# One tile fewer held as a dense adjacency: eleven dense tiles and fourteen gathered ones

## The chip, the cores and the metric

The kernel runs on one core of one Trainium2 chip. The metric is the time of one execution in microseconds of device time, median over several runs. Everything is one program: one launch, five engines (TensorE, VectorE, ScalarE, GpSimd and SyncE) that run their own instruction streams in order and wait for each other on semaphores.

## The reference

There are 3125 nodes with 256 features and 100,000 edges, each with a source, a destination and one of 4 relation types, sorted by destination. Destinations are drawn as 3125 u^2 with u uniform, so low node numbers have many edges and high ones few. What is computed, cut to what matters:

```python
X = layernorm(x)
for l in range(4):                                   # graph layers
    h = einsum('ni,rio->rno', X, W[l])               # 4 relations
    msg = h[etype, src] / max(count[dst, etype], 1)
    out = segment_sum(msg, dst) + X @ root[l] + bias[l]
    X = elu(layernorm(out) * gamma[l] + beta[l]) + X
x = x + X
x = x + mixture_of_experts(layernorm(x))             # 8 experts, the best 2 per node
```

## The kernel before, in words

The nodes are split in T = 25 tiles of TN = 125 nodes. For one tile of destinations the kernel sums source features per relation into a PSUM area of 2 x 128 partitions (the two halves of the features) x 500 columns (125 nodes x 4 relations). It has two ways to do this.

**Dense tiles** are the first NEAR = 12 tiles (line 27), which have most edges. In layer 0 their adjacency is built: 25 groups of 5 nodes per tile, each group from some slots of 128 edges. For a slot, VectorE and ScalarE make two one-hot matrices, and one matmul (`pair`, lines 1850 to 1861) multiplies them into PSUM; ScalarE copies a finished group out (line 1296). Finished tiles are stored to DRAM, and in the layers after they are loaded again in five parts each (SyncE, 625 KB a load). A tile then takes T = 25 dense steps a layer (`dense_step`, line 1872): for each tile of sources, 4 matmuls of 500 columns (line 1888; two feature halves, and a high and a low f16 part of the features).

**Far tiles** are the others. Their edges are cut in chunks of 128. For a chunk GpSimd gathers the 128 source rows of 1 KB each from DRAM by an indirect DMA (line 1421) into a ring of GS = 12 slots; VectorE makes one-hot windows for 5 chunks at a time (line 1508); TensorE does 4 matmuls, as wide as the nodes that the chunk can touch times 4 (`chunk`, lines 1895 to 1911). A slot's next gather waits until the chunk that used it is done. In layer 0 there is also one matmul per chunk that counts edges (`count`, line 1837).

How many slots and chunks a tile gets is fixed when the program is built, from the expected number of edges plus four standard deviations (`capacity`, and `self.CH`, `self.groups` in `Near.__init__`). A test at the start (`tests`) looks whether the real edges fit; if not, a second program (`DenseShape`, `dense_scalar`, `dense_tensor`) that holds all 25 tiles dense runs in place of the first. With this input the first one ran.

After a tile, of either kind, follow a scaling on VectorE (line 1601, `finish`), a split in high and low parts (lines 1312, 1523), a transpose of the tile's own features (line 1772), the relation matmuls (6 of line 1923 and 24 of line 1927), the norm and the ELU (`post`, `end`), and the new features go to DRAM (`xstore`). The gathers of a layer start when all tiles of the layer before are stored. In layer 3 the routing to the experts shares the order: per tile, GpSimd also does two scatters (line 1436).

**The order of work** on every engine is written by a planner (`Near.steps`), which keeps its own clock for each engine. The costs that bear here, in its microseconds: a dense step 0.9 on TensorE, a chunk 0.21, the relations 3.4, and a gather

```python
rows[q] = run("pool", 1.4) + 10.0      # line 537: when the rows of chunk q can be used
gather(q + GS)                         # asked for when chunk q is ordered
```

In `pick` it takes, in this order: ready jobs (relations, transposes, routing), the next chunk if it believes its rows and window there and an accumulator free, in layer 0 the next pair or count, and else the next dense step. The engines then follow this order whatever the real durations are. In layer 0 pairs run at most one tile ahead of the dense steps (line 570) and far tiles have one of the accumulator pairs to themselves; later there are three pairs for both kinds.

In `order`, the first dense tile of a layer goes through the source tiles in the order 0-4, 10-14, 15-19, 20-24, 5-9 (`groups_of`), and waits for each of them to be finished in the layer before.

Of the kernel before, what the change touches and what calls it, by code (L numbers as in the profile page):

```python
# [23 lines left out]
GD = 5  # L24
GPT = TN // GD
W = TN * R
NEAR = 12
GS = 12
OW_ = 3
FIVE = 5  # L30
# [14 lines left out]
BATCH = 4  # L45
# [31 lines left out]
S8 = 8  # L77
# [2557 lines left out]
def dense_scalar(e, a, c, m, s):  # L2635
    TD = c.TD
# [9 lines left out]
    for i in range(0, 2 * c.PT, 4):  # L2646
        n = 128 * min(4, 2 * c.PT - i)
# [7 lines left out]
    e.sem_inc(s["evac"], 4)  # L2655
    e.wait_ge(s["eg"], 32)
    e.wait_ge(s["prep"], c.prep["gp_sub"])
    regs = [e.alloc_register(f"er{TD}_{i}") for i in range(BATCH)]
    for t in range(TD):
        if t >= 2:  # L2660
            e.wait_ge(s[f"store{t % 2}"], 16 * (t // 2))
        rows = m.RA[:, 5 * (t % 2):5 * (t % 2) + 5, :].rearrange("p a b -> p (a b)").rearrange(
            "p (k q) -> p k q", q=W)
        for i in range(GPT):
            if i % BATCH == 0:
                n = min(BATCH, GPT - i)
                e.reg_load(regs[0:n], m.egrow[0:1, GPT * t + i:GPT * t + i + n])
            e.wait_ge(s["slot_free"], e.snap(regs[i % BATCH], min_val=1, max_val=c.P) + S8)
            e.activation(rows[:, :, 20 * i:20 * i + 20], m.bank((GPT * t + i) % 4, 0, W).rearrange(
                "p (q k) -> p k q", k=T), ACT.Copy).then_inc(s["evac"], 1)  # L2670

    for what, l, i in c.order:
# [14 lines left out]
        elif what == "end" and l + 1 < L:  # L2687
            t = c.done[i][1]
# [5 lines left out]
        elif what == "split":  # L2694
            n = 512 if i < E8 else 256
# [7 lines left out]
        elif what == "xo" or (what == "ra" and i + 2 < T):  # L2703
            n = i if what == "xo" else i + 2
# [371 lines left out]
def dense_tensor(e, a, c, m, s):  # L3076
    TD = c.TD
# [12 lines left out]
    e.wait_ge(s["tab"], 32)  # L3090
    e.wait_ge(s["vs"], math.ceil(c.PT / 2))
    e.wait_ge(s["prep"], c.prep["b1t"])
    regs = [e.alloc_register(f"pr{TD}_{i}") for i in range(3 * BATCH)]
    n_os = 0
    for p0 in range(0, c.P, BATCH):
        n = min(BATCH, c.P - p0)
        for w in range(3):
            at = w * c.PT * 128 + p0
            e.reg_load(regs[BATCH * w:BATCH * w + n], m.tabrow[0:1, at:at + n])
        for i in range(n):  # L3100
# [3 lines left out]
            if p % 2 == 0:  # L3104
                n_os += (p % 14 in OSG) + ((p + 1) % 14 in OSG and p + 1 < c.P)
                e.wait_ge(s["oc"], min(p + 2, c.P))
                e.wait_ge(s["os"], n_os) if n_os else None
                last = 2 * BATCH + min(i + 1, n - 1)
                e.wait_ge(s["evac"], e.snap(regs[last], min_val=1, max_val=c.G + 1))
            e.matmul(m.PS[:, bass.ds(clear, 2)], m.OS[:, p % S8, :], m.Z[:, :], start=True, stop=False,  # L3110
                     skip_group_check=True)
            e.matmul(m.PS[:, bass.ds(at, W)], m.OS[:, p % S8, :], m.OC[:, p % S8, :], start=False, stop=False,
# [171 lines left out]
```

## Time and profile before

| | us |
|---|---|
| median of 3 runs | 2614.72 |
| lowest and highest | 2608.05, 2615.36 |
| span of the profiled execution (first to last instruction) | 2581.8 |
| busy in it: TensorE | 2075.7 |
| busy in it: VectorE | 1572.2 |
| busy in it: GpSimd | 1253.4 |
| busy in it: ScalarE | 818.3 |

For the profiled execution the profile gives its span only; a full time of its own isn't listed. The median is 32.9 us above the span.
### The profile page before, as it was taken

The numbers are of one execution on the slowest core, as the hardware profiler recorded it, in microseconds if no ns is written. First come the engines' busy times: TensorE is split into PE (matmuls) and PEld (weight loads), VectorE is DVE, ScalarE is ACT, GpSimd is POOL, SyncE is SP. The second block draws the span as 40 slices with busy tenths as digits, with TensorE's granted clock in tenths as the row PEclk, the third lists the DMA queues.
The fourth block names the chain that finished last, engine by engine and source line by source line (L and its number), as shares of the span: only waits on it lengthen the run. The fifth ranks groups of instructions, "written<-read, shape, count | busy, mean of one in ns | idle before, by whom it ended". The sixth has DMA issues, their size and how long they took to land. (4 is left out here: it accounts for less than half of the span.)

```text
span 2581.8 us, 46238 instructions
## 1 busy us (share of the span) xinstructions
PE 2075.7 (80%) x16327; PEld 1296.1 (50%) x16327; DVE 1572.2 (61%) x4475; ACT 818.3 (32%) x1674; POOL 1253.4 (49%) x1223
## 2 busy tenths in 40 slices
PE   0576788787879889898889888898987988774992
PEld 0334455454545455555545545454554645454992
DVE  5976677575656356566553656566364766575665
ACT  1564556454456011111111212111011111123992
POOL 2124333544430266666716666662665656752441
PEclk9988899988889899899989999999997999986996
DMA  5698333444432487666637867765775655532335
GB/s 144 187 273 256 115 112 115 133 123 125 122 112 98 145 256 233 219 210 210 187 113 249 257 210 240 236 218 158 230 231 165 181 163 169 179 101 64 95 94 178
DMA packets 211755, 445.56 MB, mean 173 GB/s; under 512 B 40819, under 2 KB 137088, under 8 KB 209733
## 3 DMA queue, kind: packets, MB, share of 16 engines
q1 hardware_dynamic: 138357, 274.65, 34.6%
q0 software_dynamic: 61408, 156.79, 20.1%
q10 hardware_dynamic: 11760, 11.08, 1.7%
q8 instruction: 141, 2.31, 0.4%
q14 instruction: 89, 0.73, 0.1%
HBM read 338.14 MB, written 103.90 MB: 171 GB/s over the span
## 5 line engine op out<-in xcount | busy, mean ns | idle before, releaser
L1421 POOL DMA_INDIRECT n_BIG<-n_xd,n_SIDX x1080 | 1110.9, 1029 | 1091.2 <-PE n_PS L1907 501.3
L1888 PE MATMUL n_PS<-n_BIG 125*128 125x500 f16 x4800 | 1196.8, 388 | 69.3 <-issue 45.3
L1888 PEld LDWEIGHTS n_PS<-n_BIG 125*128 125x128 f16 x4800 | 441.1, 100 | 508.7 <-issue 142.0
L1907 PEld LDWEIGHTS n_PS<-n_OW,n_BIG 128*128 128x128 f16 x4320 | 256.3, 99 | 204.6 <-issue 68.9
L1907 PE MATMUL n_PS<-n_OW,n_BIG 128*128 128x84 f16 (+21 forms) x4320 | 303.5, 201 | 51.5 <-issue 41.6
L1927 PE MATMUL n_PS<-n_BIG,n_tabs 128*128 128x256 f16 x2400 | 299.3, 280 | 19.4 <-issue 18.9
L1601 DVE TENSOR_TENSOR n_ST<-n_PS,n_INVB 128x500 f32<-128x500 f32 x200 | 199.9, 1041 | 158.4 <-issue 47.6
L1927 PEld LDWEIGHTS n_PS<-n_BIG,n_tabs 128*128 128x128 f16 x2400 | 239.7, 101 | 62.9 <-issue 29.0
L1627 DVE SCALAR_TENSOR_TENSOR n_U<-n_PS,n_cw,n_BI 125x256 f32<-125x256 f32 x100 | 48.2, 482 | 334.9 <-PE n_PS L1927 161.3
L1296 ACT ACTIVATE n_BIG<-n_PS 128x500 f16<-128x500 f32 x300 | 164.3, 578 | 195.5 <-PE n_PS L1859 93.6
L1312 ACT ACTIVATE n_tabs<-n_ST 128x1000 f16<-128x1000 f32 x100 | 103.8, 1038 | 358.8 <-DVE n_ST L1601 192.3
L1508 DVE TENSOR_TENSOR n_OW<-n_io,n_tabs 128x460 f16<-128x460 f16 (+14 forms) x216 | 140.8, 657 | 119.4 <-PE n_PS L1907 59.7
L1323 ACT ACTIVATE n_U<-n_U 125x256 f32<-125x256 f32 x100 | 41.4, 414 | 506.6 <-issue 268.3
L1859 PE MATMUL n_PS<-n_BIG,n_tabs 128*128 128x500 bf16 (+4 forms) x590 | 140.8, 346 | 66.3 <-ACT n_BIG L1296 25.8
L1495 DVE TENSOR_SCALAR n_BIG<-n_io,n_tabs 128x500 bf16<-128x500 f16 (+4 forms) x590 | 154.4, 312 | 63.5 <-PE n_PS L1859 59.9
L1523 DVE TENSOR_TENSOR n_tabs<-n_ST,n_tabs 128x1000 f16<-128x1000 f32 x100 | 120.1, 1201 | 45.2 <-ACT n_tabs L1312 25.9
L1303 ACT ACTIVATE n_XT<-n_PS 128x500 f16<-128x500 f16 x100 | 58.7, 587 | 257.3 <-remote 139.8
L1441 POOL DMA_INDIRECT n_yg<-n_BIG,n_IDX x56 | 64.3, 1148 | 113.7 <-DVE n_BIG L2083 113.1
L1923 PE MATMUL n_PS<-n_RL,n_XT 128*128 128x256 f16 x600 | 88.5, 286 | 38.3 <-issue 21.5
L1277 ACT ACTIVATE n_tabs<-n_io,n_tabs 128x125 bf16<-128x125 f16 x294 | 93.2, 390 | 74.4 <-PE n_PS L1859 69.5
L1859 PEld LDWEIGHTS n_PS<-n_BIG,n_tabs 128*128 128x128 bf16 x590 | 56.8, 104 | 112.5 <-issue 38.0
L1923 PEld LDWEIGHTS n_PS<-n_RL,n_XT 128*128 128x128 f16 x600 | 57.6, 101 | 60.2 <-issue 24.2
(271 smaller groups left out, 2252.9 us busy)
## 6 DMA issues: line engine op xcount, KB each, us to landing
n_BIG<-n_a SPq DMA_DIRECT2D x175, 625.0 KB
n_a<-n_BIG SPq DMA_DIRECT2D x12, 3125.0 KB
n_xg<-n_tabs SPq DMA_DIRECT2D x53, 481.9 KB
n_INVB<-n_ind SPq DMA_DIRECT2D x100, 250.0 KB
n_BIG<-n_xd,n_SIDX POOLq DMA_INDIRECT x1080
n_BIG<-in_L_ffn_W_dram SPq DMA_DIRECT2D x32, 512.0 KB
n_xd<-n_BIG SPq DMA_DIRECT2D x75, 112.0 KB
n_whl<-n_BIG SPq DMA_DIRECT2D x16, 512.0 KB
```

What stands on the lines that cost most here:

```text
L1296: e.activation(rows[:, :, 20 * g:20 * g + 20], m.bank(4 + c.unit_of["block", i], 0, W).rearrange("p (q k) -> p k q", k=T), ACT.Copy).then_ ...
L1312: e.activation(m.SH[i % 2 if l else 0][:, 0, :, :, 0:TN], m.ST, ACT.Copy).then_inc(s["shi"], 1)
L1421: e.indirect_dma_start(m.GR[:, g % GS, :], None, m.XD[l % 2][:, :], bass.IndirectOffsetOnAxis(ap=m.SIDX[:, i:i + 1], axis=0)).then_inc(s[f ...
L1495: e.tensor_scalar(m.OC[i % S][:, at], m.io[:, at], m.VS[:, i:i + 1], None, ALU.is_equal).then_inc(s["oc"], 1)
L1508: e.tensor_tensor(m.OW[:, i % OW_, 0:n * wide].rearrange("p (c w) -> p c w", w=wide), m.io[:, 0:wide].unsqueeze(1).broadcast_to([128, n, w ...
L1523: e.tensor_tensor(lo, m.ST, hi, ALU.subtract).then_inc(s["slo"], 1)
L1601: ins = e.tensor_tensor(m.ST[:, h], m.bank(2 * p + h, 0, W).rearrange("p (n r) -> p r n", r=R), m.INVB[:, k, :].rearrange("p (n r) -> p r ...
L1859: e.matmul(m.bank(4 + c.unit_of["block", g])[:, at], m.OS[b % 3][:, i % 4, :], m.OC[i % S][:, at], start=(j == 0), stop=(j + 1 == c.groups ...
L1888: ins = e.matmul(m.bank(2 * p + h, 0, W), m.xps[l % 2][0:TN, part, D * k + 128 * h:D * k + 128 * h + 128], m.RA[0:TN, c.slot_of(n), W * (k ...
L1907: ins = e.matmul(m.bank(2 * p + h, at, c.width[q]), m.GR[:, g % GS, D * part + 128 * h:D * part + 128 * h + 128], ow, start=(first == 0 an ...
L1923: e.matmul(out, m.XT[:, f % 2, 2 * x + h, :], m.RH[:, l % 2, w, h, :], start=(x + w + h == 0), stop=False)
L1927: ins = e.matmul(out, sums[:, x, h, r, :], m.WH[:, l % 2, w, h, r, :], start=False, stop=(x == 1 and h == 1 and r == R - 1))
```

## The change

`NEAR` is 11. Tile 11 (nodes 1375 to 1499) is then a far tile: its pairs, block copies, store, loads and dense steps are not made, and chunks, gathers, windows and counts for it are. All shapes and the whole order follow from the constant, as the planner runs anew. The rest of the diff is in the second program, which isn't run with this input: its register loads in batches become single loads of a value.

```diff
-NEAR = 12
+NEAR = 11
...
-    regs = [e.alloc_register(f"er{TD}_{i}") for i in range(BATCH)]
...
-            if i % BATCH == 0:
-                n = min(BATCH, GPT - i)
-                e.reg_load(regs[0:n], m.egrow[0:1, GPT * t + i:GPT * t + i + n])
-            e.wait_ge(s["slot_free"], e.snap(regs[i % BATCH], min_val=1, max_val=c.P) + S8)
+            at = GPT * t + i
+            e.wait_ge(s["slot_free"], e.value_load(m.egrow[0:1, at:at + 1], min_val=1, max_val=c.P) + S8)
...
-    regs = [e.alloc_register(f"pr{TD}_{i}") for i in range(3 * BATCH)]
+    regs = [e.alloc_register(f"pr{TD}_{i}") for i in range(2 * BATCH)]
...
-        for w in range(3):
+        for w in range(2):
...
-                last = 2 * BATCH + min(i + 1, n - 1)
-                e.wait_ge(s["evac"], e.snap(regs[last], min_val=1, max_val=c.G + 1))
+                last = 2 * c.PT * 128 + p0 + min(i + 1, n - 1)
+                e.wait_ge(s["evac"], e.value_load(m.tabrow[0:1, last:last + 1], min_val=1, max_val=c.G + 1))
```

## Rows read from the trace of the kernel before

**Rows 1.** The page, part 1: busy us, share of the span, instructions.
```profile
PE 2075.7 (80%) x16327; PEld 1296.1 (50%) x16327; DVE 1572.2 (61%) x4475; ACT 818.3 (32%) x1674; POOL 1253.4 (49%) x1223
```

**Rows 2.** The page, part 2: busy tenths in 40 slices of the span.
```profile
PE   0576788787879889898889888898987988774992
...
POOL 2124333544430266666716666662665656752441
```

**Rows 3.** Stretches: from:to, us, busy us (instructions) per engine, granted clock, DMA share, GB/s.
```profile
150.00:865.00 715.00, 587.63 (x4180) 352.10 (x4179) 453.37 (x1395) 365.84 (x808) 266.76 (x258) 0.91 0.47 142
900.00:1312.00 412.00, 367.83 (x2917) 221.38 (x2916) 247.10 (x597) 60.09 (x93) 267.83 (x259) 0.96 0.69 214
1364.00:1778.00 414.00, 366.81 (x2948) 220.91 (x2947) 246.96 (x584) 77.23 (x110) 268.44 (x259) 0.99 0.74 231
1821.00:2316.00 495.00, 421.24 (x3193) 253.62 (x3191) 292.62 (x898) 75.22 (x136) 312.37 (x299) 0.92 0.58 176
...
795.00:838.00 43.00, 38.30 (x226) 21.75 (x227) 29.32 (x90) 26.96 (x58) 0.00 (x0) 0.98 0.29 105
```

**Rows 4.** Groups by line: instructions, busy us, mean ns, idle before and releaser.
```profile
L1421 POOL DMA_INDIRECT n_BIG<-n_xd,n_SIDX x1080 | 1110.9, 1029 | 1091.2 <-PE n_PS L1907 501.3 <-issue 242.0 <-DMA n_xd<-n_BIG 207.0
...
L1436 POOL DMA_INDIRECT n_xg<-n_tabs,n_INVA x38 | 47.3, 1244 | 44.2 <-DVE n_INVA L1724 32.6 <-issue 11.3 <-ACT n_tabs L1357 0.3
```

**Rows 5.** Timeline of GpSimd: start us, us, instruction, idle before and releaser.
```profile
1349.82 0.95 POOL L1421 DMA_INDIRECT n_BIG<-n_xd,n_SIDX  x1 [48.93 <-DMA n_xd<-n_BIG]
1351.08 0.95 POOL L1421 DMA_INDIRECT n_BIG<-n_xd,n_SIDX  x1 [0.30 <-issue]
...
1807.15 0.94 POOL L1421 DMA_INDIRECT n_BIG<-n_xd,n_SIDX  x1 [40.09 <-DMA n_xd<-n_BIG]
```

**Rows 6.** Waits of GpSimd, 900 to 1312 us: total us, times, longest.
```profile
POOL n_BIG L1421 <- PE n_PS L1907: 53.2, 52, 4.6
```

**Rows 7.** Timeline of TensorE where layers 1 and 2 end and layer 2 begins.
```profile
1312.42 0.25 PE L1907 MATMUL n_PS<-n_OW,n_BIG 128*128 128x16 f16 x4
1312.52 6.07 PE L1888 MATMUL n_PS<-n_BIG 125*128 125x500 f16 x28
...
1318.65 3.54 PE L1888 MATMUL n_PS<-n_BIG 125*128 125x500 f16 x16
...
1325.30 5.23 PE L1888 MATMUL n_PS<-n_BIG 125*128 125x500 f16 x24
...
1347.00 17.77 PE L1888 MATMUL n_PS<-n_BIG 125*128 125x500 f16 x72 [6.99 <-DVE n_BIG L1555]
1364.60 0.26 PE L1907 MATMUL n_PS<-n_OW,n_BIG 128*128 128x32 f16 x4
...
1777.64 0.25 PE L1907 MATMUL n_PS<-n_OW,n_BIG 128*128 128x16 f16 x4
```

**Rows 8.** Timeline of TensorE where layer 3 ends.
```profile
2290.46 2.69 PE L1888 MATMUL n_PS<-n_BIG 125*128 125x500 f16 x12
...
2298.38 1.44 PE L1923 MATMUL n_PS<-n_RL,n_XT 128*128 128x256 f16 x6 [4.33 <-DVE n_tabs L1523]
2299.61 5.04 PE L1927 MATMUL n_PS<-n_BIG,n_tabs 128*128 128x256 f16 x24
...
2304.90 1.40 PE L1907 MATMUL n_PS<-n_OW,n_BIG 128*128 128x108 f16 x24
...
2315.20 0.68 PE L1907 MATMUL n_PS<-n_OW,n_BIG 128*128 128x108 f16 x16
```

**Rows 9.** Timeline of TensorE where layer 0 ends and layer 1 begins.
```profile
847.68 2.78 PE L1927 MATMUL n_PS<-n_BIG,n_tabs 128*128 128x256 f16 x24
850.30 20.43 PE L1888 MATMUL n_PS<-n_BIG 125*128 125x500 f16 x96
...
882.01 4.35 PE L1888 MATMUL n_PS<-n_BIG 125*128 125x500 f16 x10 [6.90 <-DVE n_BIG L1555]
```

## The prediction

> **What bounds the kernel now.** I began with busy time per engine [rows 1]: TensorE 80%, GpSimd 49%, no engine full. The slices say where [rows 2]: TensorE is near nine tenths in the graph layers, GpSimd near 6 or 7 tenths in layers 1 to 3. The rest of the argument is about four stretches, one a layer [rows 3]. In layer 0 (150 to 865 us) TensorE is busy 587.63 of 715 us. From first to last chunk of layers 1, 2 and 3 it is busy 367.83 of 412, 366.81 of 414 and 421.24 of 495 us. TensorE sets the pace there, with little idle time. Next I read the costs per instruction [rows 4]: 1080 gathers, 270 a layer, mean 1029 ns. A full queue adds 0.30 us between gathers [rows 5], so 1.33 us each, against 412/270 = 1.53 us per chunk. GpSimd has 13% in hand, no more. Its waits for a chunk to free a ring slot in layer 1 are 53.2 us in 52 waits [rows 6], which is that margin. Last I looked at what TensorE still has to do when a layer's last chunk is done. In layer 1 the last chunk is at 1312.42 and 7 + 4 + 1 dense steps follow it; in layer 2 it is at 1777.64 [rows 7]. In layer 3 the order is reversed: the last three dense steps start at 2290.46 and 15 chunks follow them [rows 8]. So the two streams of each layer finish almost together, and the change takes work out of the one and adds it to the other.
>
> **Counts.** Tile 11 (nodes 1375 to 1499) is expected to hold 100000(sqrt(0.48) - sqrt(0.44)) = 2950 edges. `capacity` gives ceil((2950 + 217 + 32)/128) = 25 chunks, so NCH goes from 270 to 295. Each of its 25 groups has 118 edges, 2 pairs each: 50 pairs of 882 go. Per layer 25 dense steps (100 matmuls) go and 25 chunks (100 matmuls), 25 gathers and 5 windows come (54 to 59). In layer 0, 25 counts come and 25 block evacuations, one tile store and half of the 50 one-hot builds of ScalarE go. SP issues 15 loads of 625 KB fewer; gathers add 100 x 131 KB. These sizes nearly cancel on queues that are not full.
>
> **Layer 0.** Dense steps cost 20.43/24 = 0.85 us each at full clock [rows 9]: 21.3 us. Between 795 and 838 us TensorE did tile 11's 50 pairs beside tile 10's 25 dense steps and two relation groups, each 2.62 us for 24 matmuls (847.68 to 850.30) and about 0.7 for the 6 before: 43 - 21.3 - 6.6 - about 3 of transposes and waits leaves 12 us of pairs [rows 3, 9]. Together 33 us go. A chunk costs 4 x 0.05 us (24 matmuls of 108 columns in 1.40 us, [rows 8]), at 74 columns about 0.15; 25 of them and 25 one-matmul counts of about 0.1 us are 6 to 7 us. Net -26. The far stream of this layer is not the last to end now (GpSimd has nothing to do from 795 to 838, [rows 3]), but it gets a tile longer and needs a turn of its one accumulator pair more, so I leave 2 us for it: **-24**, bounds -32 (nothing of that) and -10 (the far stream ends last). VectorE's 50 one-hots and ScalarE's evacuations lay beside TensorE's work and give nothing more.
>
> **Layers 1 to 3, the mechanism.** TensorE's instructions run in the order that the planner wrote. It believes that a gather takes 1.4 us, takes a chunk as soon as it believes its rows there, and fills all time between with dense steps. So chunks stand about 1.4 planned us apart, whatever the number of dense steps. With 25 chunks more and 25 dense steps fewer, the dense steps run out before the chunks do. From there TensorE has only chunks, at the pace of the gathers. I call the part with dense steps A, the part after them B.
>
> Pace of A: the measured one per chunk, because its filling is unchanged. Length of B with n chunks: 12 are in the ring, so (n - 12) x 1.33 + 10.5 us, where 10.5 is from a gather's start to rows that can be used. The rows bound this only from above: 1349.82 to 1364.60, 14.8 us, with TensorE in dense steps until then [rows 5, 7]; from below by the 0.95 us of the instruction itself. I take 10.5, nearer to the upper row. The Trainium skill ("DMA: Bandwidth & Descriptors", section "Anatomy of one DMA — SWDGE (gpsimd) path") gives 2.0 us and bytes/436e3 us for such a DMA, an estimate of 2.3 us for 131 KB; by it each B would be 8 us shorter and the sum 24 us lower. No row here shows a gather that quick, and I don't use it.
>
> - Layer 1. 24 dense steps before the first chunk, 12 after the last: 264 on 270 chunks, 0.98 a chunk. After: 251 steps last for 257 chunks, A = 257 x 412/270 = 392 us. B has 38 chunks: 26 x 1.33 + 10.5 = 45. A + B = 437, before 412: +25. After the last chunk, now: 1312.5 to the first gather of the next layer at 1349.8, 37.3 us, of which 12 dense steps. From the last dense result it is 1326.3 (the first four of the 24 matmuls from 1325.30) to 1349.8, 23.5 us of scaling, relations, norm, store and load [rows 5, 7]. That chain stays; the 13.8 us ahead of it go. Net **+11**.
> - Layer 2. 23 steps ahead, about 7 behind: 270 on 270. After: 252 steps, 252 chunks, A = 252 x 413/270 = 386; B = 31 x 1.33 + 10.5 = 52; 438 against 413: +25. Tail 1777.7 to 1807.15 = 29.5 becomes 23.5: -6. The last tile to end is now a far one, needed only at dense step 20 of the next layer and not at step 6, so the 6.99 us wait at 1347.00 [rows 7] shrinks; rows then arrive in 12 us and not 15: -3. Net **+16**.
> - Layer 3. 276 steps on the 255 chunks until 2293, 471 us, 1.85 us a chunk (routing shares the order). After: 251 steps on 232 chunks, A = 429; B has 63: 51 x 1.33 + 10.5 = 78, and about 7 scatters of 1.24 + 0.30 us [rows 4] on the same queue, 11, and 4 for waits as in the 15 chunks that end this layer now. 522 against 494 us: +28; the same -3 for the start, and -4 because B's relation groups find their inputs ready. Net **+21**.
>
> **Sum**: -24 + 11 + 16 + 21 = +24 us. The profiled execution has a span of 2581.8 us; its own full time isn't given, and I let the 32.9 us between the span and the median 2614.72 stand. 2605.8 + 32.9 = 2639 us. Own range of this case 2612 to 2668: layer 0 by its bounds, B at 1.25 us a gather with 8 us of latency (-4, -6, -8), or at 1.45 (+4, +5, +8) with A's pace 1% off.
>
> **Rivals.**
> 1. *Other side: TensorE stays the bound everywhere.* Gathers have 13% in hand and grow 9%. If the order still had filling for all chunks, each layer would lose 21.3 us of dense steps and gain 4: -17.5 in layers 1 to 3 at the granted clock, -26 in layer 0, -79 in all, 2536 us. For it: the 53.2 us of ring waits [rows 6]. Against: the planner's own 1.4 us x 295 = 413 us is more than its work in a layer, and layer 3 shows dense work ending first already. It decides if B is under some 15 chunks a layer. 0.12.
> 2. *Break-even.* The far stream doesn't hold layer 0 (-32), B runs at 1.25 us with 8 us of latency and 15 loads fewer let A run 1 to 2% faster (4 to 7 us a layer; the 0.3 us issue gaps inside dense steps are in 412 us): -10 to -35, about 2595. 0.20.
> 3. *The clock.* Before 2298.38 TensorE waited 4.33 us and the next 24 relation matmuls took 5.04 us, against 2.78 elsewhere [rows 8]; after a 6.90 us wait, 10 dense matmuls took 4.35 us, 0.42 each and not 0.21 [rows 9], which is 1.2 and not 2.4 GHz. In B TensorE waits before every chunk. If it is at 1.2 GHz in all of B and into the next layer, 2 or 3 relation groups cost 2.9 us more each and the 24 dense steps that open a layer up to 20 us more, of which the 36 us of chain and first gather hide most: +10 to +20 a layer, 2639 + 45 = 2684. The Trainium skill's page "TensorE: Matmul & The Clock Gate", section "HAM oscillation — how this bites in real kernels", describes this: short bursts between waits for DMA keep starting on the slow clock. By that rule this rival holds; the rows show it after waits of over 4 us, not after 1 us. 0.15.
> 4. *Another program.* If tile 11's edges didn't fit its 25 chunks, the all-dense program would run, some hundreds of us slower. Room for four standard deviations makes it 0.01.
>
> **Chances.** The forecast has 0.52, of which a fifth lies within 0.3% (8 us, about what a measurement of this kernel can tell from no change). Slower: 0.42 + 0.15 + 0.01 + 0.01 of rival 2 = 0.59. Same: 0.10 + 0.06 of rival 2 = 0.16. Faster: 0.12 + 0.13 = 0.25. The range leaves out rival 1 and the upper part of rival 3: 2585 to 2680.
>
> **What would show it.** Layer 0: first gather of layer 1 at 861, not 885. Layers 1 to 3: a run of 35 to 65 chunks with no dense step between at each layer's end, gathers there 1.25 to 1.35 us apart with "issue" before them, TensorE waiting ahead of L1907 and its busy share under a half. First gathers of layers 2 and 3 465 to 480 us after those of 1 and 2 (before 465 and 457). I am wrong if dense steps still stand after the last chunk (rival 1), or if B shows relation groups of 5 us (rival 3).

## The result and the profile after

| us | before | after |
|---|---|---|
| median (4 runs each) | 2615.04 | 2672.95 |
| lowest and highest | 2608.05, 2619.2 | 2666.2, 2680.95 |
| full time and span of the profiled execution | not listed, 2581.8 | 2680.95, 2679.2 |
| granted clock over the span | 0.924 | 0.893 |

The kernel is slower: 2672.95 against 2615.04 us, +57.9, ratio 1.0237 [1.0208, 1.0266]. I had forecast +24. Only 1.75 us lie outside the span of the profiled execution after. So there is no 32.9 us around the span, as I had let stand: the profiled execution before was some 31 us quicker than the timed ones. Why is not shown. It may have run on another chip: e12 below, the same kernel of twelve tiles on a chip where it takes 2582 us, has its first gathers at 885.94, 1350.05 and 1807.69 us, within 1 us of those in that first profile. For the forecast it matters little: scaled to 2615 us, the +24 stays +24.

The busy times after, from the page's parts 1 and 2 and its groups (instructions, busy us, mean ns, idle before):

```profile
PE 2046.9 (76%) x16306; PEld 1292.4 (48%) x16306; DVE 1570.1 (59%) x4439; ACT 794.8 (30%) x1617; POOL 1351.9 (50%) x1323
...
PE   0576878778788889798579898966988898534993
...
L1421 POOL DMA_INDIRECT n_BIG<-n_xd,n_SIDX x1180 | 1210.5, 1026 | 1095.8 <-PE n_PS L1907 549.4
L1888 PE MATMUL n_PS<-n_BIG 125*128 125x500 f16 x4400 | 1102.2, 389 | 39.6 <-issue 31.2
```

Against [rows 1, 2, 4] TensorE works 28.8 us less and the span is 97 us longer. The new thing in the slices are the holes in TensorE's row, "57", "66" and "534", where before there was one, "77": they are the ends of layers 1, 2 and 3. The 100 gathers that came cost as much each as those before (1026 against 1029 ns). Where the holes are, the stretches of the kernel after show (from:to, us, busy us (instructions) of TensorE, its weight loads, VectorE, ScalarE and GpSimd, granted clock, DMA share, GB/s). For layers 1, 2 and 3 the first line is part A, the second part B:

```profile
150.00:865.00 715.00, 567.65 (x4114) 342.44 (x4114) 435.77 (x1324) 341.89 (x750) 289.79 (x283) 0.89 0.48 142
908.00:1298.00 390.00, 344.66 (x2736) 205.49 (x2735) 226.30 (x539) 54.81 (x84) 256.99 (x249) 0.97 0.70 217
1298.00:1358.00 60.00, 25.21 (x277) 20.45 (x274) 33.49 (x89) 8.24 (x14) 36.89 (x35) 0.70 0.40 109
1397.00:1765.00 368.00, 327.06 (x2555) 193.50 (x2553) 209.27 (x501) 64.16 (x91) 243.47 (x236) 0.96 0.74 230
1765.00:1850.00 85.00, 36.48 (x371) 28.30 (x370) 44.42 (x108) 12.96 (x20) 52.16 (x51) 0.68 0.43 126
1889.00:2284.00 395.00, 346.22 (x2617) 204.69 (x2618) 231.00 (x715) 58.68 (x107) 255.57 (x247) 0.93 0.61 185
2284.00:2428.00 144.00, 59.84 (x506) 45.92 (x503) 73.12 (x234) 19.50 (x38) 82.79 (x80) 0.63 0.31 84
```

Parts B exist as forecast: 44, 58 and 73 chunks with no dense step between, TensorE busy 42%, 43% and 42% of 60, 85 and 144 us. But they are longer than the 45, 52 and 93 us that I gave them. In layer 0 [rows 3] TensorE is busy 20 us less in the same 715 us. GpSimd's timeline gives the first gather of each layer; the 885, 1349.82 and 1807.15 us of before [rows 5] have become

```profile
893.33 0.95 POOL L1421 DMA_INDIRECT n_BIG<-n_xd,n_SIDX  x1 [66.78 <-DMA n_xd<-n_BIG]
...
1385.66 0.95 POOL L1421 DMA_INDIRECT n_BIG<-n_xd,n_SIDX  x1 [31.05 <-DMA n_xd<-n_BIG]
...
1877.44 0.95 POOL L1421 DMA_INDIRECT n_BIG<-n_xd,n_SIDX  x1 [31.08 <-DMA n_xd<-n_BIG]
```

Layer 0 is no shorter, and each period from first gather to first gather is longer: 492.3 for 464.9, 491.8 for 457.3. The forecast range for these was 465 to 480.

Inside part B of layer 1, TensorE's timeline (start us, us, instructions, in brackets the idle time before and its releaser):

```profile
1320.59 1.46 PE L1923 MATMUL n_PS<-n_RL,n_XT 128*128 128x256 f16 x6 [5.17 <-issue]
1321.85 4.43 PE L1927 MATMUL n_PS<-n_BIG,n_tabs 128*128 128x256 f16 x24
1326.11 2.22 PE L1907 MATMUL n_PS<-n_OW,n_BIG 128*128 128x100 f16 x48
1339.17 0.60 PE L1772 MATMUL n_PS<-n_idh,n_BIG 125*128 125x125 f16 x4 [10.84 <-issue]
...
1345.61 1.46 PE L1923 MATMUL n_PS<-n_RL,n_XT 128*128 128x256 f16 x6 [5.34 <-DVE n_tabs L1523]
1346.87 3.88 PE L1927 MATMUL n_PS<-n_BIG,n_tabs 128*128 128x256 f16 x24
1350.58 2.44 PE L1907 MATMUL n_PS<-n_OW,n_BIG 128*128 128x84 f16 x48
...
1357.89 0.27 PE L1907 MATMUL n_PS<-n_OW,n_BIG 128*128 128x16 f16 x4 [1.40 <-DMA n_BIG<-n_xd,n_SIDX]
1358.01 7.55 PE L1888 MATMUL n_PS<-n_BIG 125*128 125x500 f16 x24
```

and GpSimd's in the same place:

```profile
1323.38 0.95 POOL L1421 DMA_INDIRECT n_BIG<-n_xd,n_SIDX  x1 [0.31 <-issue]
1326.73 0.95 POOL L1421 DMA_INDIRECT n_BIG<-n_xd,n_SIDX  x1 [2.40 <-PE n_PS L1907]
...
1346.68 0.94 POOL L1421 DMA_INDIRECT n_BIG<-n_xd,n_SIDX  x1 [0.30 <-issue]
1351.17 0.94 POOL L1421 DMA_INDIRECT n_BIG<-n_xd,n_SIDX  x1 [3.55 <-PE n_PS L1907]
```

This is a loop that I had not seen. The far tiles have 25 to 18 chunks each, so in B one ends every 18 or 19 chunks. In layer 1 its transposes stand 1 to 5 chunks later in TensorE's order and its relation group 3 to 8, where the planner believes their inputs ready. In B no dense steps stand between, so TensorE waits 5 to 11 us at the head of its queue for VectorE's chain, with chunks whose rows are there behind it; then it does 12 chunks in a burst (48 matmuls in 2.22 us). For the waits of 5.17 and 10.84 us the profile names no releaser ("issue"); I put them down to VectorE because its split (line 1523, 1319.34 to 1320.54 us) and its scaling (line 1601, 1337.15 to 1339.12 us) end right before them. Meanwhile the ring of 12 slots is full and GpSimd waits 2.40 and 3.55 us for a free one. The gathers in B come 1.63 us apart, not 1.33.

### The profile page after: what moved, and what is told of

It is laid out like the page before. It is cut to its first block and busy times, and to the rows that moved or that the text cites. A ratio compares the mean times of both kernels' runs of the same rounds, so it can differ in the third digit from the quotient of the medians.

```text
span 2679.2 us, 46213 instructions
## 1 busy us (share of the span) xinstructions
PE 2046.9 (76%) x16306; PEld 1292.4 (48%) x16306; DVE 1570.1 (59%) x4439; ACT 794.8 (30%) x1617; POOL 1351.9 (50%) x1323
## 5 line engine op out<-in xcount | busy, mean ns | idle before, releaser
L1421 POOL DMA_INDIRECT n_BIG<-n_xd,n_SIDX x1180 | 1210.5, 1026 | 1095.8 <-PE n_PS L1907 549.4
L1888 PE MATMUL n_PS<-n_BIG 125*128 125x500 f16 x4400 | 1102.2, 389 | 39.6 <-issue 31.2
L1888 PEld LDWEIGHTS n_PS<-n_BIG 125*128 125x128 f16 x4400 | 403.2, 100 | 437.2 <-issue 114.1
L1907 PE MATMUL n_PS<-n_OW,n_BIG 128*128 128x76 f16 (+19 forms) x4720 | 331.4, 203 | 94.3 <-issue 79.1
L1907 PEld LDWEIGHTS n_PS<-n_OW,n_BIG 128*128 128x128 f16 x4720 | 278.1, 100 | 243.2 <-issue 107.3
L1927 PE MATMUL n_PS<-n_BIG,n_tabs 128*128 128x256 f16 x2400 | 318.9, 291 | 23.0 <-issue 22.5
L1927 PEld LDWEIGHTS n_PS<-n_BIG,n_tabs 128*128 128x128 f16 x2400 | 249.5, 105 | 78.8 <-issue 35.9
L1508 DVE TENSOR_TENSOR n_OW<-n_io,n_tabs 128x460 f16<-128x460 f16 (+16 forms) x236 | 152.7, 652 | 144.7 <-remote 83.3
L1296 ACT ACTIVATE n_BIG<-n_PS 128x500 f16<-128x500 f32 x275 | 151.5, 578 | 209.4 <-PE n_PS L1859 120.0
L1441 POOL DMA_INDIRECT n_yg<-n_BIG,n_IDX x56 | 64.5, 1151 | 112.7 <-DVE n_BIG L2083 112.1
L1772 PE MATMUL n_PS<-n_idh,n_BIG 125*128 125x125 f16 x400 | 43.5, 234 | 98.9 <-issue 59.4
L1859 PEld LDWEIGHTS n_PS<-n_BIG,n_tabs 128*128 128x128 bf16 x556 | 53.7, 105 | 125.2 <-issue 66.0
```

The lines of the kernel that those rows point to most:

```text
L1296: e.activation(rows[:, :, 20 * g:20 * g + 20], m.bank(4 + c.unit_of["block", i], 0, W).rearrange("p (q k) -> p k q", k=T), ACT.Copy).then_ ...
L1421: e.indirect_dma_start(m.GR[:, g % GS, :], None, m.XD[l % 2][:, :], bass.IndirectOffsetOnAxis(ap=m.SIDX[:, i:i + 1], axis=0)).then_inc(s[f ...
L1508: e.tensor_tensor(m.OW[:, i % OW_, 0:n * wide].rearrange("p (c w) -> p c w", w=wide), m.io[:, 0:wide].unsqueeze(1).broadcast_to([128, n, w ...
L1859: e.matmul(m.bank(4 + c.unit_of["block", g])[:, at], m.OS[b % 3][:, i % 4, :], m.OC[i % S][:, at], start=(j == 0), stop=(j + 1 == c.groups ...
L1888: ins = e.matmul(m.bank(2 * p + h, 0, W), m.xps[l % 2][0:TN, part, D * k + 128 * h:D * k + 128 * h + 128], m.RA[0:TN, c.slot_of(n), W * (k ...
L1907: ins = e.matmul(m.bank(2 * p + h, at, c.width[q]), m.GR[:, g % GS, D * part + 128 * h:D * part + 128 * h + 128], ow, start=(first == 0 an ...
```

## The experiments

The sets of runs were made on different chips, and the same kernel of twelve tiles took 2615, 2293, 2583.64, 2295.63 and 2582.57 us on them (the first is that of the result). So each ratio is against the kernel before on the same chip, and times are compared only within a set: the first is e1 to e3, the second e4 to e7, the third e8 to e11, the fourth e12 to e15. Chunk stretch means first to last chunk of a layer, tail means last chunk to the next layer's first gather.

**e1: only the second program's edit.** The diff is the kernel after with its constant put back, and e8 and e12 are this kernel again.

```diff
-NEAR = 11
+NEAR = 12
```

> NEAR stays 12; only the second program, which does not run, has the edited register loads. Theory (all of the change comes from the eleventh and twelfth tile): same as before within 0.3%, about 2615 us. Rival (the size or place of the second program's code moves instruction loading of the first): a difference of 10 us or more, either way.

2296.56 us against 2293.08, ratio 1.0017 [1.0006, 1.0027]; again as e8, 0.9999 [0.9987, 1.0012], and as e12, 0.9991 [0.9964, 1.0018]. The edit of the program that doesn't run costs nothing that the three agree on. It is all in the constant.

**e2: gathers of 64 rows**, with the order of the kernel after. Half of each chunk's edges are left out of the sums.

```diff
-            e.indirect_dma_start(m.GR[:, g % GS, :], None, m.XD[l % 2][:, :],
-                                 bass.IndirectOffsetOnAxis(ap=m.SIDX[:, i:i + 1], axis=0)
+            e.indirect_dma_start(m.GR[0:64, g % GS, :], None, m.XD[l % 2][:, :],
+                                 bass.IndirectOffsetOnAxis(ap=m.SIDX[0:64, i:i + 1], axis=0)
...
-                           m.GR[:, g % GS, D * part + 128 * h:D * part + 128 * h + 128], ow,
+                           m.GR[0:64, g % GS, D * part + 128 * h:D * part + 128 * h + 128], ow[0:64],
```

> The changed kernel, same order of work, but each gather fetches the first 64 rows of its chunk and the chunk's matmuls contract over 64 rows and not 128 (half of each chunk's edges are left out of the sums). Theory S (in the stretches without dense steps, B, the pace is that of the gathers, 1.33 to 1.63 us each): a gather gets clearly shorter, B shrinks from 60, 84 and 145 us by a third or more, and the time falls from 2673 to about 2590. Rival H (B's pace is set by relation groups that stand three chunks behind a finished tile and wait for VectorE and ScalarE, with all later chunks queued behind them): the gathers get shorter but B stays within 10 us of 60, 84, 145, and the time is 2650 to 2670.

2411.42 us (two runs), ratio 1.0515 [1.0494, 1.0536]. The manipulation failed: half the rows don't make a gather much shorter on GpSimd. The group of gathers in e2:

```profile
L1421 POOL DMA_INDIRECT n_BIG<-n_xd,n_SIDX x1180 | 1165.0, 987 | 877.7 <-PE n_PS L1907 421.6 <-issue 270.1 <-DMA n_xd<-n_BIG 121.1
```

987 ns against 1033 in e8; the median instruction is 908 ns for 64 rows and 946 for 128. So it says nothing on what cheap gathers would bring. It says that a gather's price on GpSimd hardly depends on its rows, 64 or 128. Part A became slower (1.46, 1.44 and 1.56 us a chunk) on TensorE's side: in layer 1 (799 to 1166 us) TensorE is busy 363.49 of 367 us, and 66.9 us of idle time, in 169 pieces of at most 0.4 us that no wait explains, stand before the weight loads of the 64-row chunks. Why they stand there isn't shown.

**e3: eleven tiles, the planner believes that a gather takes 1.25 us.** It then spends fewer dense steps per chunk, so more are left for later and B is shorter.

```diff
-                    rows[q] = run("pool", 1.4) + 10.0
+                    rows[q] = run("pool", 1.25) + 10.0
```

> The changed kernel with one number of the planner changed: it believes that a gather takes 1.25 us and not 1.4, so it puts fewer dense steps between two chunks and keeps more of them for the end of the layer. No work is added or removed. Theory S: TensorE's part A has slack over the gathers (1.55 us a chunk against 1.33), so it carries more chunks, B shrinks by a third and the time falls by 30 to 50 us, to about 2630. Rival H: B's stalls per finished tile stay, fewer tiles end in B, 10 to 20 us are won. A third (gathers can't go faster than in A now): no change, the waits move into A.

2334.69 us, ratio 1.0173 [1.0141, 1.0205]. That is not told apart from the kernel after (e9, 1.0211 [1.018, 1.0241]). B shrinks from 44, 58 and 73 chunks to 17, 35 and 46, yet layer 1's chunk stretch is 384.4 us as against 383.8 in e9. What B loses comes back in A, as waits for rows. In layer 1 of e3 (785 to 1149 us), waits of TensorE's weight loads and matmuls (total us, times, longest):

```profile
PEld n_PS L1907 <- DMA n_BIG<-n_xd,n_SIDX: 25.7, 26, 3.4
...
PE n_PS L1907 <- DMA n_BIG<-n_xd,n_SIDX: 17.0, 15, 3.2
```

and in e9, with the planner's 1.4:

```profile
PEld n_PS L1907 <- DMA n_BIG<-n_xd,n_SIDX: 3.0, 5, 1.3
...
PE n_PS L1907 <- DMA n_BIG<-n_xd,n_SIDX: 1.9, 4, 0.9
```

So in layer 1 it isn't how the dense steps are spread that costs; the stream of 295 chunks does. (e3 and e9 ran on two chips, on which the kernel before took 2293 and 2296 us.)

**e4: the kernel after again**, as the base of the second set; no edit.

> The changed kernel as it is, timed in the same call as the next three. In the call before, the kernel with twelve dense tiles took 2293 us where it took 2615 at first, and its trace had hardly any idle time before TensorE's instructions that nothing explains. Theory (the loss is in B, part A has room): with less such idle time A runs at the gathers' pace already (1.36 us a chunk), so the loss is larger in per cent: 2293 becomes 2360 to 2400. Rival (the loss came from the idle time of the first chip): the two kernels are within 1% of each other.

2635.53 us, ratio 1.0196 [1.0152, 1.024]. First gathers at 879.3, 1365.3 and 1856.5 us, parts B 56.8, 82.1 and 134.5 us.

**e5: twelve tiles with the planner's 1.25**, the edit of e3 on the kernel of e1.

> Twelve dense tiles and a planner that believes in 1.25 us a gather. Its order leaves 29, 31 and 22 dense steps after the last chunk of layers 1 to 3 (12, 7 and none before). If part A is bound by the gathers already (1.365 us a chunk on this chip against 1.33), nothing is won, and the tail of dense steps adds up to 17 to 24 steps of 0.85 us a layer: 2293 to 2330 us. If A had room, 2270.

2625.02 us, ratio 1.0172 [1.0136, 1.0208]. Now 29, 31 and 22 dense steps stand after the last chunk. The chunk stretches are 408.4, 403.8 and 471.5 us (1.51, 1.50 and 1.75 us a chunk), and what costs are the tails of layers 1 and 2, 50.2 and 52.7 us where the first profile has 37.4 and 29.5. A mismatch of the two streams costs about as much on the other side as the change does on this one.

**e6: eleven tiles, relation groups believed ready 5 us later** (the edit below, at both places where they are asked for), so that they stand later in TensorE's order: in part B of layer 1, 7 to 12 chunks after the end of their tile, not 3 to 8.

```diff
-                    job(max(sums[n], turned[n]), "product", l, n)
+                    job(max(sums[n], turned[n]) + 5.0, "product", l, n)
```

> Eleven dense tiles, and the planner believes the input of a relation group ready 5 us later than before, so in B it stands 6 to 9 chunks after the tile's transpose and not 2 or 3. The number of chunks in B hardly changes (45, 60, 74). Rival H (relation groups too early in the order hold up the chunks behind them and so the gathers): B's gathers come closer to 1.30 us apart, 3 to 6 us are won for each of the 2 to 4 tiles that end in B, 15 to 35 us in all against the changed kernel. Theory S alone (gather supply): within 8 us of the changed kernel.

2645.31 us, ratio 1.0232 [1.0194, 1.0269], beside e4's 1.0196 not told apart. The loop seen in B is real: the gathers there come 1.51, 1.51 and 1.72 us apart for 1.54, 1.64 and 1.97 in e4, and B of layer 3 is 115.0 us for 134.5. But the relations then end later: the tails of layers 1 and 2 are 32.5 and 32.8 us for 27.9 and 28.5, and from layer 3's last chunk to the experts' first matmul it is 57.8 us for 38.2. What the waits of the relation groups cost in B is paid elsewhere when they are moved.

**e7: ten dense tiles**, `NEAR = 10`, 322 chunks.

> Ten dense tiles: 322 chunks a layer, 275 - 25 dense steps. 112, 112 and 130 chunks of layers 1 to 3 and 37 of layer 0 stand after the last dense step, where with eleven it is 44, 58, 73 and none. Theory (a layer's length is its number of chunks at the pace of the gathers, in B 1.4 to 1.7 us, plus 40 us between layers; layer 0 gains nothing more): 27 chunks more a layer cost 27 x 1.4 = 38 us in layers 1 to 3, layer 0 gains at most 10: 100 to 120 us over the changed kernel. Rival (TensorE's work decides and B's stalls are a matter of the order's end only): 20 to 50 us over it.

2777.33 us, ratio 1.0734 [1.0694, 1.0774], 142 us over e4, above what I expected. The parts B have 112, 112 and 130 chunks. New is layer 0: 37 chunks stand behind its last dense step, 60.0 us, and the next layer's first gather is at 913.1 us, for 879.3. There the far stream ends layer 0 for certain; with eleven tiles (e4) its last chunk is 26 us ahead of the last dense step.

**e8 and e9: twelve and eleven tiles on one chip**, each with a profile, no edit beyond e1's.

> Twelve dense tiles (only the second program, which does not run, has the edited loads), for a trace taken beside that of the next kernel. Same as before within 0.3%. Theory: layers 1 and 2 from first gather to first gather as in the first trace (465 and 457 us) or, where TensorE has hardly any unexplained idle time, as in the second (408, 406).

> The changed kernel, beside the one above. Theory: against it, layer 0 gives 5 to 10 us back, layers 1 and 2 (first gather to first gather) are 20 to 35 us longer each, layer 3 up to the start of the experts 5 to 10 us longer; 50 us in all, and more, 70 to 90, if on this chip the part with dense steps has little unexplained idle time, since the gathers then bound both parts.

2294.79 and 2341.61 us, ratios 0.9999 [0.9987, 1.0012] and 1.0211 [1.018, 1.0241]. First gathers of layers 1 to 3 in e8, from GpSimd's timeline:

```profile
792.39 0.94 POOL L1421 DMA_INDIRECT n_BIG<-n_xd,n_SIDX  x1 [112.79 <-DMA n_xd<-n_BIG]
...
1198.69 0.95 POOL L1421 DMA_INDIRECT n_BIG<-n_xd,n_SIDX  x1 [44.04 <-DMA n_xd<-n_BIG]
...
1604.21 0.94 POOL L1421 DMA_INDIRECT n_BIG<-n_xd,n_SIDX  x1 [38.23 <-DMA n_xd<-n_BIG]
```

and in e9:

```profile
785.00 0.94 POOL L1421 DMA_INDIRECT n_BIG<-n_xd,n_SIDX  x1 [61.92 <-DMA n_xd<-n_BIG]
...
1210.31 0.95 POOL L1421 DMA_INDIRECT n_BIG<-n_xd,n_SIDX  x1 [30.14 <-DMA n_xd<-n_BIG]
...
1633.29 0.94 POOL L1421 DMA_INDIRECT n_BIG<-n_xd,n_SIDX  x1 [31.04 <-DMA n_xd<-n_BIG]
```

With spans of 2290.3 and 2340.1 us that is, by layer, -7.4, +19.0, +17.5 and +20.7, in all +49.8. The chunk stretches, divided by 270 and 295 chunks, are the plainest number of the case:

| us per chunk | layer 1 | layer 2 | layer 3 |
|---|---|---|---|
| before, profile of the forecast | 1.53 | 1.53 | 1.83 |
| after, first profile | 1.53 | 1.53 | 1.83 |
| e8, twelve tiles | 1.31 | 1.34 | 1.51 |
| e9, eleven tiles | 1.30 | 1.30 | 1.51 |
| e12, twelve tiles | 1.53 | 1.53 | 1.84 |
| e14, eleven tiles | 1.50 | 1.51 | 1.75 |
| e7, ten tiles (322 chunks) | 1.54 | 1.49 | 1.71 |

The time per chunk hardly changes when dense steps are taken away: it falls by 0 to 5%. On the chip of e8 and e9 TensorE is full where it has dense steps: in part A of layer 1 of e9, 799 to 1132 us, it is busy 328.60 of 333.00 us (1.32 us a chunk). But the order spends about one dense step per chunk there whatever is left of them, and in B only the pace of the gathers counts (1.30 and 1.34 us apart in layers 1 and 2), so what was taken from TensorE is not got back. TensorE's pace in A is the planner's choice of filling; that it nearly equals the gathers' pace in B on this chip is no law.

**e10: twelve tiles, the planner believes that a gather takes 1.46 us.** The opposite edit to e5, from what the others pointed to: spend the dense steps a little earlier, so that none stands behind the last chunk.

```diff
-                    rows[q] = run("pool", 1.4) + 10.0
+                    rows[q] = run("pool", 1.46) + 10.0
```

> Twelve dense tiles and a planner that believes in 1.46 us a gather: 2, 2 and 36 chunks of layers 1 to 3 stand after the last dense step, and no dense step after the last chunk (with 1.4: 12, 7 and none dense steps after, 15 chunks in layer 3). Theory (what costs is a stretch in which one of the two streams runs alone): layers 1 and 2 win 5 to 10 us each at their end, layer 3 loses 10 for 21 chunks more without filling: within 0.5% of before. Rival (only the gathers' pace counts, any wider spacing of the chunks costs its 0.06 us x 270 a layer): 30 to 45 us slower.

2280.51 us, ratio 0.9937 [0.9914, 0.9959]: the only version that beats both kernels. 2, 2 and 36 chunks stand after the last dense step. The first gather of layer 2 is at

```profile
1188.27 0.94 POOL L1421 DMA_INDIRECT n_BIG<-n_xd,n_SIDX  x1 [33.53 <-DMA n_xd<-n_BIG]
```

and so layer 1 takes 399.3 us for 406.3 in e8: its chunk stretch is 5 us longer (359.3) and its tail 12 us shorter (25.8 for 37.5). Layer 2 takes 403.3 us for 405.5, layer 0 ends 3.4 us earlier, and the rest from layer 3 on is 1 us longer.

**e11: eleven tiles, each of the 175 chunks of parts B multiplied four times**, to keep TensorE working there.

```diff
+    for again in range(4 if (l, q) in c.tail else 1):
...
-                           start=(first == 0 and part == 0), stop=False, skip_group_check=True)
+                               start=(first + again == 0 and part == 0), stop=False, skip_group_check=True)
```

> The changed kernel, but every chunk that stands after a layer's last dense step (175 in layers 1 to 3) is multiplied four times and not once, so its edges are counted fourfold. 12 more matmuls of about 90 columns a chunk, 0.5 us, 85 us of work in all for TensorE, in the stretch where it waits. Clock theory (the waits let TensorE fall to 1.2 GHz, relation groups take 4 to 5 us and not 2.8, and this feeds back into the chunks behind them): work in the gaps keeps 2.4 GHz, relation groups in B take 3 us, and the time is the same or up to 15 us less. Rival (the slow clock hides behind the gathers, or the work adds to the chain): 5 to 30 us more than the changed kernel. If TensorE were the bound in B: 85 us more.

2346.87 us, ratio 1.0219 [1.0187, 1.025], not told apart from e9. Part B of layer 1 in e9:

```profile
1132.00:1184.00 52.00, 26.62 (x268) 20.61 (x269) 31.67 (x82) 8.23 (x14) 36.90 (x38) 0.73 0.48 134
```

and in e11:

```profile
1135.00:1184.00 49.00, 42.13 (x729) 38.24 (x726) 30.65 (x76) 7.83 (x13) 36.61 (x37) 0.90 0.49 137
```

The granted clock rises from 0.73 to 0.90, and the parts B are 54, 76 and 121 us for 52, 72 and 120. On this chip neither the clock nor TensorE's work in B sets its length; the gathers, 1.29 us apart in B of layer 1, do. The edit raises both at once, so a small gain by the clock could hide behind the added work. On the chips of the forecast, where the gathers in B wait for TensorE and are 1.63 us apart, it wasn't tried.

**e12 to e15: what holds layer 0.** e12 and e14 are the kernels of twelve and of eleven tiles; e13 and e15 are the same with three of four matmuls left out of 46 dense steps of layer 0.

```diff
+    thin = l == 0 and t >= c.TD - 2 and 0 < kk < T - 1
     for h in range(2):
         for part in range(2):
+            if thin and (h, part) != (1, 1):
+                continue
```

> The kernel with twelve dense tiles again, as the base of the next run on the same chip. Ratio to the kernel before 1.00. Its first gather of layer 1 marks where layer 0 ends (792.4 us on a quicker chip, 885.0 on the first).

> Leaves out part of the computation: in layer 0, the 23 middle dense steps of tiles 10 and 11 do one of their four matmuls, so TensorE has 138 matmuls of 0.213 us (29.4 us) less there, and all else stays: the order, one-hots, copies, windows, the far stream. Theory A, that which my forecast used (TensorE's work is what layer 0 takes): layer 0 and the whole kernel are 27 to 29 us shorter. Theory B (removing TensorE's work there leaves more waits for VectorE, ScalarE and the far stream): 10 to 20 us shorter, and the idle time of TensorE in layer 0 grows by the rest.

> The kernel after again, as the base of the next run on the same chip. Ratio to the kernel before 1.02; its layer 0 ends 6 to 8 us before that of the twelve-tile kernel (7.4 and about 6 in two comparisons), where the forecast had 24.

> The same cut in the kernel after: the 23 middle dense steps of tiles 9 and 10 do one of four matmuls in layer 0, 29.4 us of TensorE's work less. Theory A (work alone): 27 to 29 us shorter than the kernel after. Theory B (in this kernel the far stream with its one accumulator pair, a tile longer, and VectorE's finishes are nearer to being the last of layer 0): the gain is smaller than the same cut brings with twelve tiles, 5 to 15 us. If both cuts bring the same, the far tile more is not what holds layer 0, and what was wrong there is the amount of TensorE's work.

| | median us | ratio to before | last pair of layer 0 | its last dense step ends | first gather of layer 1 |
|---|---|---|---|---|---|
| e12, twelve | 2581.57 | 0.9991 [0.9964, 1.0018] | 835.3 | 866.6 | 885.9 |
| e13, 29.4 us of matmuls fewer | 2575.34 | 0.9966 [0.9949, 0.9984] | 834.0 | 851.6 | 881.9 |
| e14, eleven | 2641.39 | 1.0226 [1.0201, 1.0251] | 836.4 | 869.6 | 888.7 |
| e15, 29.4 us of matmuls fewer | 2626.37 | 1.0164 [1.014, 1.0188] | 831.3 | 851.4 | 883.0 |

(The last dense step is found by counting matmuls along the planned order.) With 29.4 us of TensorE's work out, layer 0 ends (first gather of layer 1) 4.0 us earlier with twelve tiles and 5.7 with eleven. So theory A falls, and e13 gives less than even theory B had. Both cuts bring nearly the same, so the far tile more isn't what holds layer 0 either. The last pair comes within 5.1 us in all four, though e14 and e15 have 50 pairs fewer. (The medians fall by 6 and 15 us. What e15 gains beyond layer 0 lies in layer 2, 475.4 for 484.3 us, where nothing was edited; a layer of one profile varies by that much.) Stretches of e12 with tile 11's pairs (first line) and up to the next layer (second):

```profile
740.00:836.00 96.00, 87.32 (x554) 51.14 (x555) 64.86 (x203) 58.12 (x127) 10.08 (x9) 0.95 0.33 105
836.00:886.00 50.00, 39.48 (x207) 20.40 (x205) 22.42 (x58) 7.40 (x11) 0.06 (x1) 0.92 0.51 144
```

and of e13:

```profile
740.00:836.00 96.00, 80.81 (x513) 47.45 (x511) 66.71 (x210) 61.08 (x133) 12.49 (x12) 0.95 0.34 109
836.00:882.00 46.00, 29.63 (x136) 15.37 (x137) 21.57 (x59) 6.98 (x10) 0.14 (x1) 0.70 0.46 156
```

In the first of these stretches waits came where the work went from. TensorE's waits for ScalarE's copy of a finished block there, e12:

```profile
PEld n_PS L1859 <- ACT n_BIG L1296: 1.5, 4, 0.7
...
PE n_PS L1859 <- ACT n_BIG L1296: 0.3, 1, 0.3
```

and e13:

```profile
PEld n_PS L1859 <- ACT n_BIG L1296: 13.6, 21, 2.0
PE n_PS L1859 <- ACT n_BIG L1296: 6.0, 7, 1.5
```

TensorE is busy 91% of that stretch in e12 and still its work isn't what sets the length: pair, copy, free PSUM and next pair form a loop over TensorE and ScalarE, with the one-hots of VectorE beside it, and the dense steps lay in its gaps. That this loop sets the length is argued from these waits, not shown: e14 and e15 have 50 pairs fewer and no earlier last pair to match.

Behind the last pair it is otherwise. There the cut in the last tile's steps, 14.7 us, comes through: the last dense step ends 15.0 us earlier in e13 and 18.2 in e15. But 11.0 and 12.5 us of that are lost before the next layer's first gather. TensorE's timeline in e12:

```profile
871.54 0.38 PE L1772 MATMUL n_PS<-n_idh,n_BIG 125*128 125x125 f16 x4
...
873.30 2.78 PE L1927 MATMUL n_PS<-n_BIG,n_tabs 128*128 128x256 f16 x24
```

and in e13:

```profile
861.31 1.84 PE L1891 MATMUL n_PS<-n_BIG 125*128 125x500 f16 x4 [5.48 <-DVE n_BIG L1555]
863.21 0.60 PE L1772 MATMUL n_PS<-n_idh,n_BIG 125*128 125x125 f16 x4
...
867.01 4.99 PE L1930 MATMUL n_PS<-n_BIG,n_tabs 128*128 128x256 f16 x24
```

A dense step of layer 1 stands in the order ahead of the last tile's transposes and waits 5.48 us for the features of another tile, and the relation group runs at a lower granted clock (0.70 over the stretch): its 24 matmuls take 4.99 us, not 2.78.

## Why the prediction was off, step by step

The direction and its mechanism hold: dense steps run out, a part B of chunks alone ends each layer, and the time goes up. The size forecast, +24, was less than half of the measured +57.9. By layer (to the end of the span for layer 3):

| us | forecast | first profiles | e8 to e9 | e12 to e14 |
|---|---|---|---|---|
| layer 0 | -24 | +8.4 | -7.4 | +2.7 |
| layer 1 | +11 | +27.5 | +19.0 | +22.3 |
| layer 2 | +16 | +34.4 | +17.5 | +26.7 |
| layer 3 and after | +21 | +27.1 | +20.7 | -0.4 |
| sum | +24 | +97.4 | +49.8 | +51.3 |

The sum of the first pair holds the 31 us by which the profile before was quicker than its timed runs and the 8 us by which the profile after was slower than its median; the two may be of different chips, so the other two pairs are the sounder ones. The medians say +58, +46 (e8, e9) and +60 (e12, e14).

- **Layer 0, -24: the step that failed, and the largest part of the miss.** I priced the edit as TensorE's work, because TensorE was busy 587.63 of 715 us [rows 3]. Much of the work went as counted: between 150 us and layer 0's last dense step TensorE is busy 558.5 us of 623 in e8 and 540.3 of 616 in e9, -18 for -26. But its idle time grew from 64.5 to 75.7, and the layer ended 7.4 us earlier, not 24; in e12 to e14 it ended 2.7 us later. What grew are the waits of pairs for ScalarE's copy, in e8 and then in e9 (150 to 770 us):

```profile
PE n_PS L1859 <- ACT n_BIG L1296: 14.0, 11, 8.6
...
PE n_PS L1859 <- ACT n_BIG L1296: 18.7, 17, 3.6
```

Without one wait near 267 us, which e9 has too (10.3 us, put down to a window), the 14.0 us are 5.4. So the copies, which I had let lie beside TensorE's work for nothing, are part of what paces the layer, and e13 and e15 show that 29.4 us of TensorE's work in its last two dense tiles are worth 4 to 6. A busy share of 82% isn't a bound. What the bound of the layer is, is not shown as a whole: the copy loop while pairs run, and the order behind the last pair, are what the traces point to. Of my bounds (-32, -10) even the near one is outside, and -32 doesn't follow from its terms, which give -26 with nothing for the far stream. That the far stream ends last, my reason for -10, isn't so with eleven tiles; it is with ten.
- **Counts.** 295 chunks, 1180 gathers, 4400 dense matmuls, 160 loads: all as worked out. The pairs that went made TensorE busy 7.4, 9.9 and 11.9 us less in the three pairs of profiles (150 to 885 us), for 12.
- **Part A, pace unchanged**: right within 2%. 1.55 us a chunk (1.53 forecast) up to the last dense step in layers 1 and 2, 392 us forecast for layer 1, 389.8 measured. Its length in layers 2 and 3 was mis-sized: 35 dense steps, not 24, stand before the first chunk there, since the far tiles end last and the next layer's dense work has begun in the tail. So 12 fewer are left, and B has 58 and 73 chunks, not 43 and 63.
- **Part B, (n - 12) x 1.33 + 10.5**: the form is right and the 1.33 too low on the chips of the forecast. With the real n it gives 53, 72 and 92 us (and 116 with the 16 scatters of layer 3). e9 has 52, 72 and 120. The first profile has 60, 84 and 145, since gathers wait for ring slots behind TensorE's waits for the relations (1.63 us apart). The stretches grow by 38, 40 and 46 us for +25, +25 and +28 (30, 23 and 38 in e8 to e9; 31, 32 and 18 in e12 to e14). The waits of 5 to 11 us, and what they do to the ring, were not in the sum; nor were 9 of the 16 scatters, as I had counted 7.
- **The 10.5 us of latency**: in the first profile after, TensorE waited for the rows of the last three gathers of layers 1 and 2 and had them 3.22, 3.72 and 4.21 us, and 3.12, 3.62 and 4.17 us, after each gather's start. In e9, over layers 1 to 3, the rows TensorE waited for took 3.4 us in the median and 2.69 at the quickest; in e3, where TensorE waits for rows in part A too, the median is 5.5 and the longest 12.4. So 10.5 was far too long for the end of a layer. The 2.3 us, an estimate by the Trainium skill ("DMA: Bandwidth & Descriptors", section "Anatomy of one DMA — SWDGE (gpsimd) path"), which I set aside, is nearer, though no gather here was that quick. My 10.5 held only because it stood for time that B loses otherwise.
- **Tails**: -13.8 and -6 forecast; -9.6 and -1.7 measured (27.8 us each, not 23.5). The start in layers 2 and 3: -3, measured -3.6 and -3.2. Ahead of the experts: -4 for an edge that is worth 14.5 us in e8 to e9 (53.7 to 39.2 us). That layer 3 comes out at +20.7 there for my +21 is luck: its stretch grew by 38 us, not 28, and the edge hid it.
- **The range**: its upper end, 2668, doesn't follow from its own terms; +14, +17 and 1% of 1207 us of part A give 2682.
- **Rival 1** (TensorE the bound everywhere) falls: it decided below some 15 chunks in B, and there are 44 to 73. Layer 1 of e3, with 17 chunks in B, comes nearest to its condition, and that layer isn't quicker than e9's. **Rival 2** falls by layer 0. **Rival 3** (the clock): a lowered clock in B is real (granted 0.63 to 0.70 there in the first profile after), with relation groups of 3.88 and 4.43 us for 2.78 in layer 1; my sign for it, groups of 5 us, shows once in that layer of e9 (4.99 us). But e11 gives the clock back and gains nothing on its chip, and the dense steps that open layer 2 lost some 2.4 us (the first 24 matmuls took 7.55 us, at full clock 5.1), not up to 20. The Trainium skill's rule of the oscillating clock ("TensorE: Matmul & The Clock Gate", section "HAM oscillation — how this bites in real kernels") holds as a description of B; it says that short bursts between waits for DMA start on the slow clock, and the trace agrees, with granted clocks of 0.70, 0.68 and 0.63 in the three parts B, where the waits are for VectorE as well. That it costs nothing is shown by e11 for its chip alone. **Rival 4** didn't happen.

Open: what TensorE's unexplained "issue" gaps are (in layer 1 of the first profile before it is idle 44.2 of 412 us, 40.2 of them "issue"; in e8 6.8 of 355 us, none), with which the same layer takes 1.53 us a chunk on some chips and 1.31 on others; what bounds layer 0; and why layer 3 costs +20.7 and +27.1 in two pairs and nothing in the third.

## What to carry to other kernels

Where two streams of a stage end together, take the time of the stage per unit of each stream, and try the forecast "time per unit stays, number of units goes up" first. For layers 1 to 3 it gives +38, +38 and +46 us a stretch; 38, 40 and 46 came in the first pair and less, 31, 32 and 18, in e12 to e14. With e8's figures it gives 33, 33 and 38, and 30, 23 and 38 came. It is a guide for an order with fixed spacing like this one, and not more. An engine that is busy 80 or 90% of a stretch isn't yet its bound; take a known amount of its work out (29 us here, worth 4 to 6) before a gain is priced at its busy time, and look where the rest of it went. And where the streams are balanced by a planner, try its constants too: with twelve tiles, one of them moved from 1.4 to 1.46 brought 15 us (0.6%).

## What the runs showed of the hardware that I had not expected

A gather on GpSimd costs 0.95 us with 128 rows (e8, median) and 0.91 with 64 (e2), with 0.30 us between two; where TensorE waited for its rows in e9, they were there 3.4 us after its start in the median (2.7 to 9.9). The same program took 2293 to 2296 us on some chips and 2583 to 2615 on others, with the same instructions: layer 1 takes 1.31 us a chunk on the first kind (e8) and 1.53 on the other (e12).
